# Four transformer layers on one core: up to four query products share a PSUM bank and are emptied together

## The reference, cut to what matters

```python
x = x + xattn(layernorm(x), ctx)      # layers 0, 1, 2, 3, then the feed-forward part of each
q = layernorm(x) @ Wq (+ bq)          # 112 x W
k = ctx @ Wk (+ bk);  v = ctx @ Wv (+ bv)   # 375 x W
s = q_h @ k_h.T * scale               # 112 x 375 for each head h
out = softmax(s (masked in layers 0 and 3)) @ v_h
# layer 0: 16 heads of 16 (W = 256), mask, biases     layer 1: 1 head of 256 (W = 256), biases
# layer 2: 16 heads of 64 (W = 1024)                  layer 3: 16 heads of 16 (W = 256), mask
```

## Time and profile before

| what | us |
|---|---|
| median of 3 runs (2906.94 to 2907.54) | 2907.07 |
| the profiled execution's own time | 2910.14 |
| its span | 2908.3 |
| TensorE busy in the span (89%) | 2584.1 |
| VectorE busy in the span (47%) | 1354.4 |
| ScalarE busy in the span (37%) | 1089.5 |
| TensorE's mean granted clock | 0.938 |

### The profile page before, as it was taken

How to read it: one execution, slowest core, us unless ns; L and a number is a source line. 1 busy time by engine, 2 the same in 40 slices (tenths; PEclk the granted TensorE clock), 3 DMA queues, 4 the chain that set the end, 5 groups by cost and what they waited for, 6 DMA issues and landing times.

```text
span 2908.3 us, 45464 instructions
## 1 busy us (share of the span) xinstructions
PE 2584.1 (89%) x15668; PEld 2098.1 (72%) x15668; DVE 1354.4 (47%) x4098; ACT 1089.5 (37%) x2870; POOL 214.3 (7%) x245
## 2 busy tenths in 40 slices
PE   5999996999889779949999999999869689999993
PEld 4999995777656557647777777778657469999862
DVE  5667663222244532254444444444432456666504
ACT  3666661222121112214333333333212157777610
POOL 0000000111000024200000000000024200000000
PEclk8999997999989879969999999999969879999997
DMA  6776655222241112310000000000042377776300
GB/s 185 172 171 165 168 139 209 73 87 87 69 162 42 56 31 65 87 40 12 6 15 9 12 10 15 6 15 4 9 176 65 85 191 167 167 167 167 80 0 26
DMA packets 147727, 248.02 MB, mean 85 GB/s; under 512 B 14704, under 2 KB 124608, under 8 KB 144832
## 3 DMA queue, kind: packets, MB, share of 16 engines
q1 hardware_dynamic: 136560, 214.95, 27.6%
q0 software_dynamic: 10944, 30.16, 3.4%
HBM read 186.07 MB, written 58.98 MB: 84 GB/s over the span
## 4 chain that ended last, share of the span: by engine, by line
PE 86%; DVE 9%; DMA 1%; ACT 1%; issue 1%; SPq 0%; DVEq 0%; ACTq 0%; POOLq 0%; PEldq 0%
PE bank L791 15%; PE bank L774 9%; PE bank L1435 8%; PE bank L1465 5%; PE bank L705 5%; PE bank L698 5%; PE bank L694 5%; PE bank L1490 5%; PE bank L709 4%; PE bank L762 4%; PE bank L685 4%; PE bank L757 4%; PE bank L721 3%; PE bank L1478 3%; PE bank L1738 2%; PE bank L1724 2%
## 5 line engine op out<-in xcount | busy, mean ns | idle before, releaser
L791 PE MATMUL bank<-arena 125*112 125x64 f32 (+4 forms) x4704 | 555.6, 258 | 0.9 <-DVE on L988 0.6
L791 PEld LDWEIGHTS bank<-arena 125*112 125x112 f32 x4704 | 519.5, 178 | 5.1 <-issue 0.7
L774 PEld LDWEIGHTS bank<-ident,arena 112*125 112x125 f32 x2352 | 341.3, 188 | 86.6 <-issue 69.8
L774 PE MATMUL bank<-ident,arena 112*125 112x112 f32 x2352 | 369.2, 274 | 0.2 <-DVE arena L1017 0.2
L1004 DVE CUSTOM_DVE_ANT_0 arena<-bank,maskf 112x375 f32<-112x375 f32 x512 | 279.0, 545 | 157.5 <-PE bank L757 150.9
L1043 ACT ACTIVATE arena<-arena,mx 112x375 f32<-112x375 f32 x512 | 309.6, 605 | 101.0 <-DVE mx L1004 100.5
L1008 DVE TENSOR_REDUCE mx<-bank 112x1 f32<-112x375 f32 x272 | 137.3, 544 | 297.2 <-PE bank L762 290.8
L1043 ACT ACTIVATE arena<-bank,mx 112x375 f32<-112x375 f32 x272 | 153.8, 570 | 289.0 <-DVE mx L1008 288.1
L757 PE MATMUL bank<-kS,qS 128*112 128x376 f32 x512 | 236.0, 461 | 15.2 <-DMA kS<-key_halves 15.2
L1435 PE MATMUL bank<-arena 128*128 x552 | 240.4, 558 | 3.4 <-ACT arena L1537 3.2
L1017 DVE COPY arena<-bank 125x336 f32<-125x336 f32 x400 | 202.2, 506 | 73.1 <-PE bank L791 58.4
(11 more groups left out here) (207 smaller groups left out, 3423.3 us busy)
## 6 DMA issues: line engine op xcount, KB each, us to landing
kS<-key_halves SPq DMA_DIRECT2D x256, 188.0 KB, 5.5
qS<-query_halves SPq DMA_DIRECT2D x128, 224.0 KB, 4.8
arena<-in_ctxT SPq DMA_DIRECT2D x64, 376.0 KB, 4.1
key_halves<-arena SPq DMA_DIRECT2D x64, 376.0 KB, 5.0
arena<-in_f_out SPq DMA_DIRECT2D x22, 768.0 KB, 4.4
query_halves<-arena SPq DMA_DIRECT2D x32, 448.0 KB, 2.8
arena<-in_f_up SPq DMA_DIRECT2D x4, 2816.0 KB, 19.5
arena<-results SPq DMA_DIRECT2D x20, 448.0 KB, 8.4
```

Source lines behind the costliest of these rows:

```text
L774: m = pe.transpose(bank[2 + g % 2][0:KT, k * S:(k + 1) * S], pr[:, g % t.NR, k * KT:(k + 1) * KT], ident[0:S, 0:S])
L791: m = pe.matmul(bank[ob][0:S, col:col + wide], pTv[:, g % 2, k, :], Vv(t, b)[:, k, h * dh:h * dh + wide], start=(k == 0), stop=(k == NKT - 1))
```

## The change

A new number `QG = min(4, NO)` is the size of a group of q pieces: 4 in layer 2, 2 in the others. One gen now makes QG pieces, one behind the other, in neighbouring 112-column stretches of one bank (448 of its 512 columns in layer 2, 224 elsewhere). In layer 2 one VectorE instruction of 448 columns empties the group. In layers 0, 1 and 3 the bank is still emptied by two VectorE instructions, as before, but only the last of them signals; the first now waits for the whole group. So a batch has 2 q gens instead of 8 in layer 2, and 1 instead of 2 elsewhere. The matmuls are the same, in number and shape.

```diff
--- before.py
+++ after.py
@@ -128,6 +128,7 @@
         self.lag, self.NR = (3, 3) if self.stack else (2, 3) if self.halves else (2, 2)
         self.NV, self.NS = (8, 8) if self.H == 1 else (2, 2)
         self.moe = L < 3
+        self.QG = min(4, self.NO)
         self.G = B * self.H
         self.plan = self.numbered(self.steps())
         self.gens = [s for s in self.plan if s[0] == "gen"]
@@ -158,7 +159,7 @@
     def proj(self, b):
 
         gen = lambda kind, o, h=0: ("gen", kind, b, o, h)
-        q = [(gen("q", o), 0.45, 0) for o in range(self.NO)]
+        q = [(gen("q", o), 0.45 * self.QG, 0) for o in range(0, self.NO, self.QG)]
         k = [(gen("k", o), 1.0 if self.halves else 1.26, 0) for o in range(self.NO)]
         v = [(gen("v", kt, h), 1.37 if self.halves else 0.86, 0) for kt in range(NKT) for h in range(self.VH)]
         if self.stack:
@@ -681,9 +682,10 @@
                 if n >= 2:
                     freed(pe, t, n - 2)
                 if kind == "q":
-                    for c in range(ND):
-                        m = pe.matmul(dst[:, 0:S], w[0][:, c, o * P:(o + 1) * P], xnT[:, c, b * S:(b + 1) * S],
-                                      start=(c == 0), stop=(c == ND - 1))
+                    for j in range(t.QG):
+                        for c in range(ND):
+                            m = pe.matmul(dst[:, j * S:(j + 1) * S], w[0][:, c, (o + j) * P:(o + j + 1) * P],
+                                          xnT[:, c, b * S:(b + 1) * S], start=(c == 0), stop=(c == ND - 1))
                 elif t.halves and kind in "kv":
                     if o == 0 and kind == "k":
                         pe.wait_ge(t.halved, 4 + 2 * (b + 1))
@@ -748,9 +750,10 @@
                     if h == 0 and t.stack:
                         pe.wait_ge(t.stacked[b % 2], STACK_DMAS[0] * (b // 2 + 1))
                     elif h == 0:
-                        for kind in "qk":
-                            for o in range(max(0, t.NO - 2), t.NO):
-                                freed(pe, t, t.gen_index(kind, b, o))
+                        for o in range(0, t.NO, t.QG):
+                            freed(pe, t, t.gen_index("q", b, o))
+                        for o in range(max(0, t.NO - 2), t.NO):
+                            freed(pe, t, t.gen_index("k", b, o))
                     if g >= 2:
                         pe.wait_ge(t.maxed if t.masked else t.probs, t.h0 + g - 1)
                     if t.stack:
@@ -868,7 +871,6 @@
                 a = queries if part == 0 else keys[:, :, part - 1:part, :]
                 if part == 0:
                     freed(dve, t, t.gen_index("q", b, 0))
-                    freed(dve, t, t.gen_index("q", b, 1))
                 else:
                     freed(dve, t, t.gen_index("k", b, part - 1))
                 at = b * 6 + part * 2
@@ -888,21 +890,25 @@
 
                     if b:
                         dve.wait_ge(t.stacked[(b - 1) % 2], STACK_DMAS[0] * ((b - 1) // 2 + 1))
-                    out = queries[:, 0, o, :].rearrange("p (e s) -> p e s", e=2)
-                    q2 = src[:, 0:S].unsqueeze(1).broadcast_to([P, 2, S])
                     by_parity = sel2[:, :].unsqueeze(2).broadcast_to([P, 2, S])
-                    if t.a["bq"]:
-                        ins = dve.scalar_tensor_tensor(out=out, in0=q2, scalar=biasA[:, 0, o:o + 1],
-                                                       in1=by_parity, op0=ALU.add, op1=ALU.mult)
+                    for j in range(t.NO):
+                        out = queries[:, 0, j, :].rearrange("p (e s) -> p e s", e=2)
+                        q2 = src[:, j * S:(j + 1) * S].unsqueeze(1).broadcast_to([P, 2, S])
+                        if t.a["bq"]:
+                            ins = dve.scalar_tensor_tensor(out=out, in0=q2, scalar=biasA[:, 0, j:j + 1],
+                                                           in1=by_parity, op0=ALU.add, op1=ALU.mult)
+                        else:
+                            ins = dve.tensor_tensor(out, q2, by_parity, ALU.mult)
+                elif kind == "q":
+
+                    if H == 1:
+                        for j in range(t.NO):
+                            ins = dve.tensor_scalar(qmv(t, b)[:, j, :], src[:, j * S:(j + 1) * S],
+                                                    biasA[:, 0, j:j + 1], qscale, ALU.add, ALU.mult)
                     else:
-                        ins = dve.tensor_tensor(out, q2, by_parity, ALU.mult)
-                elif kind == "q":
-
-                    if H == 1:
-                        ins = dve.tensor_scalar(qmv(t, b)[:, o, :], src[:, 0:S], biasA[:, 0, o:o + 1],
-                                                qscale, ALU.add, ALU.mult)
-                    else:
-                        ins = dve.tensor_scalar(qmv(t, b)[:, o, :], src[:, 0:S], qscale, None, ALU.mult)
+                        ins = dve.tensor_scalar(qmv(t, b)[:, o:o + t.QG, :],
+                                                src[:, 0:t.QG * S].rearrange("p (o t) -> p o t", t=S),
+                                                qscale, None, ALU.mult)
                 elif kind == "v":
                     ins = dve.tensor_tensor(Vv(t, b)[:, o, h * t.VW:(h + 1) * t.VW],
                                             src[0:KT, 0:t.VW], bvB[0:KT, :], ALU.add)
```

## The result

The changed kernel took 2859.45 us (median of 4 runs, 2858.18 to 2863.47). The kernel before took 2907.01 us in 4 runs (2904.76 to 2907.54). The ratio is 0.984, with a 95% interval of 0.9823 to 0.9857: 47.6 us less. The forecast was 33.4 us less, and its low end of 2865 us was too high. The direction and the places were right, the size was not.

A forecast was written before the change was run, and what follows sets the result against it. The prediction took TensorE, busy 89% of the span, to bound the kernel, with savings where it waits for banks. From the 2907.1 us median, 19.4 + 3.0 + 2.6 + 4.1 + 3.3 + 0 + 1.0 = 33.4 gave 2874 us, range 2865 to 2887.

The forecast's parts named there:

- Then 24 records run in 3.28 us, 0.137 us each.: Layer 2 batches: after the wait, 24 q records take 0.137 us each, so each group of 16 takes 2.2 us.
- the term "19.4": Layer 2, batches 1 to 14: the q products' waits for VectorE, 1.39 us each, go whole, 19.4 us.
- Batch 0: Layer 2, batch 0: the 1.63 us wait and the slow stretch of 1.4 us behind it go, 3.0 us.
- Layer 2, start: Start of layer 2: k starts 4.7 us earlier but at the low clock, saving 2.6 us, bounds 0 and 4.7.
- Layer 1: Layer 1, between q and k: waits for n's emptying and the first q emptying go, 4.1 us, bounds 1.9 and 4.3.
- The clock term: Layer 1: four clock drops of 1.7 us each, 6.8 together; half taken as gone, 3.3 us, bounds 0 and 6.8.
- Layers 0 and 3, batches: Layers 0 and 3: first emptying 0.5 us later, covered by idle time; cost nothing, bounds 0 and 15 us.
- Layer 0, start: Start of layer 0: the first k product gets its own bank, saving 1.0 us, bounds 0 and 2.1.
- no emptying came through in layers 0 and 3: Rival, layers 0 and 3: the later emptying costs 0.5 us in 30 batches, 15 us, so 2889 us; chance 0.06.
- no wait moved to the reduction: Rival, layer 2: the wait moves to the reduction behind the second group, 2893 us if all 19.4 return; chance 0.04.
- nothing got slower: Rival, layers 0 and 3: the 0.5 us stall also drops the clock, 66 us in 30 batches, 2940 us; chance 0.03.
- The rule about the clock: Skill's rule: short idle times as banks are cycled swing the clock; drops would go with bank waits, 36.8 us in sum.

## Why the prediction missed, step by step

*What bounds the kernel.* Right: TensorE waited once per layer 2 batch for the context split, and that wait went whole (19.4 us).

*"Then 24 records run in 3.28 us, 0.137 us each."* This is the step that failed. The figure was read as TensorE's pace, and the new q phase was sized by it ("16 x 0.137"). It was the pace of the two-bank ring, 1.06 us for two pieces. TensorE's own is 3.61 / 32 = 0.113. So the term "19.4" for batches 1 to 14 of layer 2 was too small. The pitch of a batch fell by 2.0 us (49.6 to 47.6 in one batch, 50.8 to 48.7 in the next): 1.39 is the idle row of the wait, 0.25 the part of the same wait that no idle row shows, and 0.34 two hold-ups of the ring. Over 14 batches that is 28 us where 19.4 were counted. Of the 8.6 that were missed, 4.8 is the ring and some 3.5 the hidden part of the wait. The prediction took a wait to cost what its idle row says. Of the ring there was a sign in the rows quoted: VectorE's last emptying stood idle for 0.17 us waiting for a q piece.

*Batch 0.* Predicted 3.0, measured 31.9 - 28 = 3.9 us. The whole slow stretch went, as said, and the ring and the wait's hidden part with it. The timeline to compare with the earlier trace rows:

```profile
1294.79 3.83 PE L687 MATMUL bank<-xnT,arena 128*128 128x112 f32 x32
1298.55 0.89 PE L765 MATMUL bank<-arena 64*112 64x375 f32 x4
```

*Layer 2, start.* Predicted 2.6, measured 2.7. k waits 7.07 us for VectorE where about 6 were reckoned, and it starts at the low clock, as expected. Counted from the layer's LN transposes it starts 4.8 us earlier (4.7 reckoned), and the k records start 0.313 us apart at the low level (0.31 reckoned) and 0.171 at the high one. So the term came out by its mechanism; that the low level would end where it ended before was assumed, and it did (27.0 us behind the LN transposes, 27.1 before). The timeline, and a window of 2 us in it (the clock is the third figure from the end):

```profile
1273.99 1.15 DVE L909 TENSOR_SCALAR arena<-bank 128x448 f32<-128x448 f32 x2
1274.66 10.51 PE L696 MATMUL bank<-ctx_halves,weight_halves 128*128 128x376 f32 x45 [7.07 <-DVE arena L909]
```

```profile
1277.00:1279.00 2.00, 2.00 (x8) 2.00 (x8) 0.00 (x0) 0.66 (x2) 0.00 (x0) 0.50 1.05 451
```

*Layer 1.* Waits 4.1 predicted, 4.5 by difference (11.3 less four drops of 1.7). The clock term is the second one that was mis-sized: half of 6.8 us was taken as a hedge, all of it went in this run, and the 11.3 us together lie above the 4 to 10 that the prediction named as the sign of being right. The kernel with the 0.48 us wait put back shows that the drops depend on it; over the other kernels some 0.7 drops stay, so 5.6 us on average would have been the right size.

*Layers 0 and 3, batches.* Right at nothing: 0.8 us more and 0.8 us less; first to last scores of layer 0 took 391.2 and 391.4 us with groups of one and 391.2 to 392.4 with groups of two. The 0.5 us delay of the first emptying is hidden, as argued.

*Layer 0, start.* Predicted 1.0, measured 1.4. *Layer 1 and 3, start:* 1.9 and 0.9 not predicted; of the first, 1.6 came with layer 1 unchanged, by a clock that rose 3 us sooner; why it did stays open. Of the 0.9, all that is known is that the start of layer 3 took 25.6 to 25.7 us in the two kernels with groups of one there and 23.3 to 25.3 in the others; the cause stays open.

Together the stages save 50.1 us and the spans differ by 50.9, of which 3.07 was the profiled run of before being above its median. So what counts is 47.6 between medians against 33.4. What is above the forecast is 8.6 us in batches 1 to 14 of layer 2, 3.9 in layer 1, 0.9 in batch 0, 3.3 at the four starts and 0.8 outside the table, and the 3.07 goes off again: 14.4 for the 14.2. The smaller of these are less than the stretches that no edit touches differ by from run to run (276.1 to 280.4 us from layer 1's last scores to the next LN transposes).

*The rivals.* None came: no emptying came through in layers 0 and 3, no wait moved to the reduction, nothing got slower. The range failed because all of it took the 19.4 us of idle rows and the ring's pace as they stood; its low end added only the clock and the starts.

*The rule about the clock.* The granted clock dropped in 10 places over the three kernels with 2.1 us of idle time in layer 1, and in 7 over the ten with 1.64. The Trainium skill, TensorE: Matmul & The Clock Gate, section "A second HAM failure mode: psum-queue depth-cycling", ties such drops to short idle times as banks are cycled; the trace agrees in layer 1, and in layer 2 of the kernel before 1.39 us dropped it in none of 14 batches. Taking all of layer 1's drops as gone, as the prediction worked out by that rule, would have given 36.8 us, nearer than the forecast.

## What to carry to other kernels

Where a producer goes through a ring of two banks with short pieces, don't take its time per instruction for its own pace: here the ring cost 0.17 us at every second piece and showed as no wait of TensorE's matmuls, only as a consumer that idles 0.17 and 0.34 us in turn. Look at the distance between the starts of single records, or at the weight loads. Size a group so that every bank it needs was last used by earlier work than its own batch; groups of two left an idle row of 0.64 us in each batch, which cost 0.25 us more than it says, and groups of four none. A merged instruction on an engine that isn't waited for is worth nothing by itself.

## What the runs showed of the hardware

An idle time per batch of 1.39 us in layer 2 dropped TensorE's clock in none of 14 batches of the kernel before but in two of the kernel with only the other layers changed. One of them in its timeline, where 24 records take 4.64 us instead of 3.28:

```profile
1694.42 4.64 PE L687 MATMUL bank<-xnT,arena 128*128 128x112 f32 x24 [1.41 <-DVE arena L910]
```

In batch 0 of layer 2, 1.6 us was followed by a drop of 3.4 us in both of these kernels. 3.7 us dropped it in every batch, for 3.4 or 6.8 us. In layer 1, 1.64 us followed by 0.48 us dropped it in 3 or 4 batches of a kernel, 1.64 alone in 0 to 2. A low stretch can also come up far from any edit: the one of 10.2 us in the last batches of layer 2 came with the same order of work that had none in the changed kernel.

Signals from TensorE behind every piece and fulfilled waits ahead of them left the q phase at 3.76 us to the hundredth. A q record starts 0.112 us behind the one before and lasts 0.275, so the first 0.16 us of a hold-up count as busy time of TensorE, and so does the 0.09 us by which the first record behind it delays the next: 14 x 0.6 = 8.4 us of the 18.8 by which it fell.
